# Placing a GNN layer's node sums by node, and multiplying two blocks at once in every second step

## The reference

```
for l in range(4):
    e   = edge_attr @ We[l] + be[l]                 # (40000,1) @ (1,512)
    m   = relu(x[src] + e)                          # gather one row for each edge
    agg = segment_sum(m, dst)                       # add the rows of a target node
    h   = ((1 + eps[l]) * x + agg) @ W1[l] + b1[l]
    h   = (h - mean(h)) * rsqrt(var(h) + 1e-5) * gamma[l] + beta[l]   # over all nodes
    x   = relu(relu(h) @ W2[l] + b2[l])
out = layernorm(x0 + x)
```

## Time and profile before

| | |
|---|---|
| median of three runs | 1293.48 us |
| profiled execution, time | 1292.47 us |
| its span, first to last instruction | 1290.6 us |
| TensorE matmul busy | 1208.2 us, 94% of the span |
| VectorE busy | 1035.8 us, 80% |
| GpSimd busy | 783.6 us, 61% |
| ScalarE busy | 553.5 us, 43% |

### The profile page before, as it was taken

How to read it: one execution, slowest core, us unless ns; L and a number is a source line. 1 busy time by engine, 2 the same in 40 slices (tenths; PEclk the granted TensorE clock), 3 DMA queues, 4 the chain that set the end, 5 groups by cost and what they waited for, 6 DMA issues and landing times.

```text
span 1290.6 us, 26518 instructions
## 1 busy us (share of the span) xinstructions
PE 1208.2 (94%) x7483; PEld 771.6 (60%) x7483; DVE 1035.8 (80%) x2134; ACT 553.5 (43%) x1159; POOL 783.6 (61%) x831
## 2 busy tenths in 40 slices
PE   2887999999999999999998999999998999999997
PEld 2884566666655566666654566665554566666653
DVE  7978888888876978887776978887767888888777
ACT  1923344434364444434355444444345434343343
POOL 0055677677706777777715777777714777777720
PEclk9558899999999999999999999999999999999999
DMA  3156677677736777777746777777745777777752
GB/s 113 56 186 194 193 205 218 197 209 211 232 111 200 216 218 216 217 217 218 235 136 199 215 217 217 217 217 217 234 146 185 215 217 217 218 216 215 221 190 107
DMA packets 92578, 254.23 MB, mean 197 GB/s; under 512 B 19902, under 2 KB 23114, under 8 KB 92428
## 3 DMA queue, kind: packets, MB, share of 16 engines
q0 software_dynamic: 65600, 215.01, 56.5%
q1 hardware_dynamic: 25804, 36.42, 8.6%
q10 hardware_dynamic: 1024, 1.05, 0.3%
HBM read 239.24 MB, written 12.97 MB: 195 GB/s over the span
## 4 chain that ended last, share of the span: by engine, by line
POOL 42%; PE 29%; issue 15%; DVE 10%; DMA 2%; ACT 0%; ACTq 0%; DVEq 0%; POOLq 0%
POOL rows L827 42%; PE y_ps L2106 10%; PE y_ps L1985 6%; PE pair_ps L1932 4%; DVE rows L1543 3%; DVE rows L1429 2%; PE h_ps L2063 1%; PE y_ps L2117 1%; DMA rows<-node_table,src_fast 1%; PE h_ps L1858 1%; DVE src_onehot L1360 1%; PE uT_ps L2016 1%; DMA node_table<-rows 1%; PE pair_ps L2049 1%; PE uT_ps L2023 1%
## 5 line engine op out<-in xcount | busy, mean ns | idle before, releaser
L827 POOL DMA_INDIRECT rows<-node_table,src_fast x820 | 780.9, 952 | 453.3 <-issue 248.2
L1543 DVE SCALAR_TENSOR_TENSOR rows<-We_ps,negw_fast,rows 128x512 f32<-128x512 f32 x820 | 566.3, 744 | 81.6 <-DMA rows<-node_table,src_fast 81.2
L1985 PE MATMUL y_ps<-table_parts,src_onehot 128*128 128x512 f32 x1664 | 428.7, 409 | 22.0 <-DVE table_parts L637 8.0
L1985 PEld LDWEIGHTS y_ps<-table_parts,src_onehot 128*128 128x128 f32 x1664 | 291.3, 190 | 191.2 <-issue 88.0
L1003 ACT ACTIVATE rows<-y_ps 128x512 f32<-128x512 f32 x416 | 248.7, 598 | 217.7 <-PE y_ps L1985 207.2
L1932 PE MATMUL pair_ps<-rows,onehot 128*32 128x512 f32 x2504 | 306.2, 601 | 15.0 <-DVE rows L1543 14.8
L1360 DVE TENSOR_TENSOR src_onehot<-y_ps,src_bc 126x256 fp32r<-126x256 f32 x376 | 150.8, 417 | 64.2 <-PE y_ps L1985 63.9
L1932 PEld LDWEIGHTS pair_ps<-rows,onehot 128*32 128x32 f32 x2504 | 67.4, 109 | 149.5 <-issue 112.2
L2063 PEld LDWEIGHTS h_ps<-uT,W_sb 128*128 128x128 f32 x1152 | 135.5, 194 | 6.1 <-issue 3.4
L2063 PE MATMUL h_ps<-uT,W_sb 128*128 128x128 f32 x1152 | 136.4, 278 | 0.0
L2106 PE MATMUL y_ps<-rows,hT 128*128 128x512 f32 x288 | 124.5, 594 | 0.0
(11 more groups left out here) (251 smaller groups left out, 793.3 us busy)
## 6 DMA issues: line engine op xcount, KB each, us to landing
late_rows<-node_table SPq DMA_DIRECT2D x1536, 2.0 KB
rows<-node_table,src_fast POOLq DMA_INDIRECT x820, 3.7
b_bc<-node_table ACTq DMA_DIRECT2D x512, 2.0 KB
node_table<-rows SPq DMA_DIRECT2D x29, 256.0 KB, 3.6
src_onehot<-near_ws SPq DMA_DIRECT2D x416, 2.0 KB
x_now<-x_pad SPq DMA_DIRECT2D x10, 512.0 KB, 7.7
W_sb<-W SPq DMA_DIRECT2D x4, 1024.0 KB, 5.5
rows<-W SPq DMA_DIRECT2D x16, 256.0 KB
```

The lines of the kernel that those rows point to most:

```text
L827: nc.gpsimd.indirect_dma_start(rows[:, slot, :], None, table[:, :], bass.IndirectOffsetOnAxis(src_fast[:, t:t + 1], 0)).then_inc(landed[q] ...
L1543: last = nc.vector.scalar_tensor_tensor(rows[:, slot, :], We_ps[:, :], negw_fast[:, t:t + 1], row, ALU.mult, ALU.max)
L1985: last = nc.tensor.matmul(y_ps[k % 2][:, :], src_onehot[:, 2 * (k % ONEHOTS) + b, :], table_parts[:, part, 2 * pair_of(k) + b, :], start=( ...
```

## The change

**Placing by node, blocks 0 to 7.** `place_block`, behind quad 1, makes the node sums untransposed: `place` is the stationary operand (32 columns) and a whole 512-column pair sum the moving one, six products in four groups of 32 output rows, two of which add onto groups already written (five products for block 0). VectorE adds them to `u` (`add_sums`, behind the messages of quad 3), and `turn_block`, behind quad 3, transposes the sum with four transposes. Block 8 and 9 stay as they were.

**Two blocks at once.** Blocks are multiplied in twos, in even steps 2, 4, 6 and 8, with 256 columns: `product_of_two` for the first two chunks of output behind quad 3 and for the other two behind quad 5. Of `uT`, half lies in `uT` and half in columns of `hT` that blocks 8 and 9 take later, so ScalarE copies it in two halves (`finish_one_of_two`). ScalarE adds the bias in `finish_h_of_two`, and VectorE takes the statistics of two blocks in odd steps, behind quads 4 and 5 (in the last step quads 7 and 5).

**Other places.** ScalarE scales `u` between near tiles, and keeps the carry once the block is placed. `place_w` stands behind quad 2 instead of 1.

```diff
         def rest_of_last(l):
             return y_ps[TILES_A_LAYER % 2][:, 0:D // 2].rearrange("p (c n) -> p c n", n=P)
+        node_sums = turned_uT
+
+        LATE = GUARD - MARGIN + (BLOCKS - 2) * P
+
+        def two_blocks(k):
+            return (uT[:, 2 * k:2 * k + 2, :].rearrange("p m n -> p (m n)") if k < C // 2
+                    else hT[:, k, LATE:LATE + 2 * P])
+
+        def one_of_two(i):
+            return (uT[:, :, :].rearrange("p (k m) n -> p k m n", m=2)[:, :, i % 2, :],
+                    hT[:, C // 2:C, LATE + P * (i % 2):LATE + P * (i % 2) + P])
+
+        def h_of_two(c):
+            return h_ps[:, 2 * (c % 2):2 * (c % 2) + 2, :].rearrange("p m n -> p (m n)")
+
         def sums_of(c, l, i):
             return rest_of_last(l)[:, c - C // 2, :] if i == BLOCKS - 1 and c >= C // 2 else uT_ps[:, c, :]
...
             def scale_u(n, i):
-                if n:
-                    act.wait_ge(u_turned, n)
+                if i == BLOCKS - 1:
+                    act.wait_ge(u_turned, n // BLOCKS * (BLOCKS - BY_NODE) + i - BY_NODE)
+                elif n:
+                    act.wait_ge(block_summed, n + 1)
                 nc.scalar.activation(u[:, :], x_now[:, i, :], ACT.Identity, scale=eps1[:, 0:1]).then_inc(u_scaled, 1)
             def slow_scale_u(n, i):
...
                 act.wait_ge(block_summed, n + 2)
                 act.wait_ge(h_summed, n + 1)
                 nc.scalar.copy(uT[:, :, :], uT_ps[:, :, :]).then_inc(uT_copied, 1)
+
+            def finish_one_of_two(n, i):
+
+                act.wait_ge(block_summed, n + 2)
+                if i % 2 == 0:
+                    act.wait_ge(h_summed, n + 1)
+                first, rest = one_of_two(i)
+                nc.scalar.copy(first, uT_ps[:, 0:C // 2, :])
+                nc.scalar.copy(rest, uT_ps[:, C // 2:C, :]).then_inc(uT_copied, 1)
+
+            def finish_h_of_two(n, i):
+
+                at = P * (i - 1) + GUARD - MARGIN
+                for h in range(2):
+                    act.wait_ge(h_summed, n + 1 + h)
+                    for c in range(2 * h, 2 * h + 2):
+                        last = nc.scalar.activation(hT[:, c, at:at + 2 * P], h_of_two(c), ACT.Identity,
+                                                    bias=vec[:, 0, c:c + 1])
+                    last.then_inc(h_copied, 1)
             def finish_h(n, i):
...
                         scale_u(n, i)
                     if i == 1:
                         act.wait_ge(We_rows, 64 * (l + 1))
+                    if 0 < i <= BY_NODE:
+                        act.wait_ge(block_placed, BY_NODE * l + i)
+                        keep_carry()
                     if 0 < i:
-                        finish_block(n - 1)
-                        nc.scalar.copy(carry[:, :], pair_sb[:, 1, :]).then_inc(carry_copied, 1)
-                    if i < BLOCKS - 1:
+                        if i < BLOCKS - 1:
+                            finish_one_of_two(n - 1, i - 1)
+                        else:
+                            finish_block(n - 1)
+                    if i > BY_NODE:
+                        keep_carry()
+                    if i == 0:
                         scale_u(n, i)
                     copy_pair(0, n, quad_summed[3], n + 2)
                     for q in range(0 if i else 3, 4):
                         make_tiles(l, first + q)
+                        if q == 1 and i < BLOCKS - 1:
+                            scale_u(n, i)
                     fetch_rows(l, i, 2)
                     fetch_rows(l, i, 3)
-                    if 0 < i:
+                    if i == BLOCKS - 1:
                         finish_h(n - 1, i - 1)
+                    elif i and i % 2 == 0:
+                        finish_h_of_two(n - 1, i - 1)
                     if i == 0:
                         for q in (4, 5, 6):
                             make_tiles(l, first + q)
...
                                                           ALU.mult, ALU.add)
                 last.then_inc(bn_ready, 1)
+            def add_sums(n, l, i):
+
+                dve.wait_ge(u_ready, n + 1)
+                dve.wait_ge(block_placed, BY_NODE * l + i + 1)
+                nc.vector.tensor_tensor(u[:, :], node_sums, u[:, :], ALU.add).then_inc(u_whole, 1)
+
             def kept_stats(i):
                 for c in range(C):
                     last = nc.vector.bn_stats(stats[:, c, i, :], hT[:, c, P * i:P * (i + 1)])
...
                         messages(q, l, i)
                         if i == 4 and q == 3:
                             negate_gamma(l)
+                        if q == 3 and 0 < i <= BY_NODE:
+                            add_sums(n - 1, l, i - 1)
                         if q == (3 if i < BLOCKS - 1 else 2) and l == 0:
                             keep_w(i).then_inc(w_sum_ready, 1)
                             dve.wait_ge(w_sum_ready, i + 1)
-                        if i > 2 and q == (4 if i < BLOCKS - 1 else 7):
+                        if i > 2 and i % 2 and q == (4 if i < BLOCKS - 1 else 7):
                             dve.wait_ge(h_copied, n)
                             kept_stats(i - 1)
+                        if i > 4 and i % 2 and q == 5:
+                            dve.wait_ge(h_copied, n)
+                            kept_stats(i - 2)
                         if q == 5 and i < BLOCKS - 1 and l == 0:
                             w_onehots(i + 1)
                         if q == (6 if i < BLOCKS - 1 else 2):
...
                         pe.wait_ge(pair_copied[q // 4], n + 1)
                         pe.wait_ge(onehot_ready, 2 * n + q // 4 + 1)
                     sum_quad(q, l, i)
+                    if q == 3 and 0 < i and not final:
+                        turn_block(n - 1, l, i - 1)
                     if q == 0 and l == 0 and final:
                         place_w(i)
                     if final:
...
                         for place in range(QUADS * i + q + 1 - GROUP[i], QUADS * i + q + 1):
                             gather_tiles(l, place)
                     if 0 < i:
-                        if q == (0 if final else 1):
+                        if final and q == 0:
                             open_block(n - 1, l, i - 1, True)
                             add_first_pair(n - 1, l, i - 1)
-                        if q == 1:
+                        if final and q == 1:
                             close_block(n - 1, i - 1)
-                        if q == (2 if final else 3):
+                        if not final and q == 1:
+                            place_block(n - 1, l, i - 1)
+                        if final and q == 2:
                             product_h(n - 1, l, i - 1)
+                        if not final and i % 2 == 0 and q in (3, 5):
+                            product_of_two(n - 1, l, i - 1, q == 5)
                     if q == 0 and l == 0 and i == 0:
                         sum_w(0)
-                    if q == 1 and l == 0 and not final:
+                    if q == (2 if i else 1) and l == 0 and not final:
                         place_w(i)
                     if q == 3 and final:
                         open_block(n, l, i, True)
...
+            def place_block(n, l, i):
+
+                pe.wait_ge(uT_copied, n + 1)
+                pe.wait_ge(place_ready, n + 1)
+                pe.wait_ge(pair_copied[0], n + 2)
+                pe.wait_ge(pair_copied[1], n + 2)
+                if i:
+                    pe.wait_ge(carry_copied, (BLOCKS - 1) * l + i + 1)
+                nodes = [slice(g * WIN, (g + 1) * WIN) for g in range(P // WIN)]
+                for g in range(PLACED // WIN):
+                    nc.tensor.matmul(node_sums[nodes[g], :], place0(i)[:, nodes[g]], pair_sb[:, 0, :],
+                                     start=True, stop=g == 1 or g == 0 and not i)
+                nc.tensor.matmul(node_sums[nodes[3], :], place1(i, WIN, 2 * WIN), pair_sb[:, 1, :], start=True, stop=True)
+                if i:
+                    nc.tensor.matmul(node_sums[nodes[0], :], place1(i - 1, HALF, PLACED), carry[:, :],
+                                     start=False, stop=True)
+                nc.tensor.matmul(node_sums[nodes[2], :], place1(i, 0, WIN), pair_sb[:, 1, :],
+                                 start=False, stop=True).then_inc(block_placed, 1)
+
+            def turn_block(n, l, i):
+
+                pe.wait_ge(u_whole, BY_NODE * l + i + 1)
+                for c in range(C):
+                    last = nc.tensor.matmul(uT_ps[:, c, :], u[:, c * P:(c + 1) * P], ident[:, :],
+                                            start=(c == 0), stop=True, is_transpose=True, skip_group_check=True)
+                last.then_inc(block_summed, 1)
+
             def close_last(n, l, i):
                 for h, copied, count in ((0, pair_copied[1], n + 2), (1, rest_copied, l + 1)):
...
                 for c in range(C):
                     for k in range(C):
```

(19 more changed lines are left out.)

## The result

The changed kernel takes 1322.94 us (median of four runs, 1320.2 to 1328.73) against 1291.41 us of the kernel before (four runs, 1288.86 to 1293.76). The ratio is 1.0238, with a 95% interval of 1.0202 to 1.0274: slower, near the forecast of 1318. The profiled execution took 1321.29 us with a span of 1319.4.

A forecast was written before the change was run, and what follows sets the result against it. Bound by TensorE and VectorE in turn in layer 0, near the gathers' pace in layers 1 to 3. Layer 0 12.5 + layers 1 to 3 9 + clock 3 = 24.5 us more, so 1318 us; range 1291 to 1336.

The forecast's parts named there:

- The step that decided it: Layer 0: an odd step's product is hidden, so removing it gives nothing; an even step gets 3.37 us more.
- VectorE's piece: Odd step of layer 0: VectorE's unbroken work from weight sum to quad 7's messages, 14.4 us before, near 15.2 after.
- layer 0: Its steps: even ones +2.8 us, odd ones +0.4, pairs 3.2 longer, step 1 and the last unchanged; +12.5 in all.
- its share of the clock: TensorE's clock falls once a layer after idle time in odd steps, 0.85 us each, +3 us in sum.
- the layers 1 to 3: A pair of steps takes 53.5 us, 1.6 more, over the gathers' 51.3; +3 us a layer, +9 in all.
- Placing: Eight blocks a layer: placing takes 1.85 us, with transposes 2.44 against 3.22, so 0.78 us less.
- Products: Even steps: 32 instructions of 256 columns take 6.94 us for two blocks, instead of 7.14.
- its cover: TensorE's quads 2 and 3, 1.85 us, hide VectorE's addition of node sums; without them it costs 0.7.
- The bound of GpSimd never waiting there: Layers 1 to 3: gathers still find their slots free, 1.25 us apart, and GpSimd waits for no sums.
- rival B: The gathers' pace hides all added work in layers 1 to 3: 1305 us, chance 0.22.
- Rival C: TensorE's clock falls in each of the twelve odd steps, 1.4 us each: 1331 us, chance 0.15.

The follow-up runs named there:

- gaps filled: The changed kernel plus idle 512-column products in TensorE's odd-step gaps (six and two in layer 0, two and two elsewhere): 1318.86 us, ratio 1.0219.
- the statistics spread: The changed kernel with the statistics of a pair's second block moved from the odd step to the next even step: 1315.1 us, ratio 1.0213.
- both remedies: The changed kernel with second-block statistics moved to the next even step and fewer idle products in odd-step gaps (four and one in layer 0): 1310.91 us, ratio 1.0173.

## Why the prediction was right, and which terms were off

The step that decided it held: the product of an odd step had been hidden beside VectorE's piece, and in an even step it is on TensorE's path. The run with the products alone shows all of the loss, the run with the placing alone a gain of 0.28%, and the run with the odd products cut no gain from taking the hidden work out.

That the total came so near owes something to luck. The sum of 24.5 us is 28.8 between the two profiled executions and 31.5 between the medians, and it is made of errors that partly cancel: layer 0 was forecast 9.2 us too short with its share of the clock, the layers 1 to 3 came 2.6 us under their steps and clock together, and step 0 and the end behind the last edge stage were 2.8 us shorter, which nothing in the forecast had.

- Placing: forecast 1.85 us and 0.78 less with the transposes. Measured 1.7 us on the path; with the wait for the weight copies an even step gains 0.4 to 0.6. Right, a little too dear.
- Products: 6.94 forecast, 3.45 + 3.69 = 7.14 measured.
- VectorE's piece: 15.2 us forecast, 15.4 measured. The addition behind the placing takes 690 ns and found its cover.
- Layers 1 to 3: +9 us for the steps and 0.85 for the clock in each, 11.6 in all; measured 4.5 + 1.8 + 2.7 = 9.0 for both. The bound of GpSimd never waiting there held, and rival B, which had nothing there, is out. But that 9.0 equals the forecast for the steps alone is chance, as the clock fell behind five of the nine odd steps. From the step lengths above, an estimate is 1.4 us for each even step that a fall reached, 7 us in all. At full clock less is left, 6.7 us with gaps filled and 3.5 with the statistics spread as well. With the statistics spread and five falls left it is 3.5, too, so these runs do not tell how the 9.0 divides.
- The term that was mis-sized is layer 0: +12.5 us for its steps and 0.85 for the clock, against 22.6 measured. Of the 10.1 us that the steps were short, the clock has 7.7: 5.1 in the even steps, by the run with filled gaps, and 2.6 in the odd steps 3, 5 and 7, by the run with both remedies. Rival C, a fall in each of twelve odd steps, had this for layer 0 and for five of nine odd steps behind it, eight of its twelve. The Trainium skill (TensorE: Matmul & The Clock Gate, HAM oscillation) describes a kernel whose waits between bursts of matmuls, there for DMA, put the engine back to half rate each time; the stretches at 0.50 behind TensorE's waits for VectorE agree with it in layer 0, while in the layers 1 to 3 four of nine odd steps had no fall.
- Another 4.2 us, some 1.05 in each even step at full clock, are seams which I had set to nothing. In the kernel before, quads 4 to 6 and the weight sum run through in 2.84 us, as its timeline of TensorE shows:

```profile
234.26 2.78 PE L1932 MATMUL pair_ps<-rows,onehot 128*32 128x512 f32 x24
236.86 0.37 PE L1906 MATMUL h_ps<-w_parts_cur,hT 128*32 128x3 bf16 x21
237.10 0.64 PE L1932 MATMUL pair_ps<-rows,onehot 128*32 128x512 f32 x4
```

  After, the same takes 1.85 + 0.17 + 1.00 + 0.14 + 0.36 = 3.52 us around the second lot, 0.7 more; the products are 0.2 dearer than forecast, and the last 0.2 I did not trace.
- The rest is the 1.6 us by which step 1 was shorter, which I had left as it was: 7.7 + 4.2 - 1.6 = 10.3, against 10.1. At full clock the odd steps come out as forecast, +1.1 us in sum against +1.2, though I had given step 3 the statistics of two blocks and it has those of one.
- GpSimd's waits in layer 0, 14 instead of 7, are a consequence: its slots come free late in the longer steps. In the other layers it waits for no sum, as forecast.

## What to carry to other kernels

Work that lies in another engine's shadow is free where it is; before it is gathered into fewer steps, ask for each step whether the engine has that much room, since a step that three engines end nearly together takes an addition in full and returned next to nothing for a removal. Count also what the freed gap does: here it let TensorE's clock fall at the end of the step, and the next, already longer step began at half rate. Where the gap stayed, a few idle products in it, fewer than it holds, were worth more than the time they took: with the statistics spread, the steps 1 to 9 of layer 0 took 247.1 us with them and 253.7 without.

## What the runs showed of the hardware

- Less work was slower: with 12 of 16 products taken out of three steps in ten, out of a gap, the kernel's ratio to the kernel before went from 0.9972 to 1.0047 (1286.08 and 1294.35 us), and a stretch behind the gap ran at 0.51 of the clock.
- Products of 32 columns by 512 of different accumulations run side by side as those of one quad do: the quad behind the placing started two of its eight instructions 0.86 us after the placing's first. The placing's twelve instructions cost 1.7 us.
- TensorE's clock fell to 0.50 at 269.6 us, 0.85 us behind an idle time of 4.37 us. In the layers 1 to 3 the odd steps 5 and 7 all have the same two waits, of 1.5 and 1.7 us, and the clock fell beside four of the six. In the kernel before, one fall followed an idle 1.77 us, while 2.66 us was followed by none.
